# Sums on TensorE in sixteen uneven groups, and two units of a chunk moved from rows to columns

## The reference

```python
e = stack([tbl_f[ids[:, f]] for f in range(32)], axis=1)       # 1024 x 32 x 64
z = einsum('bne,hne,bnh->bn', e[:, ROW], K, e[:, COL])         # 1024 x 496
h = concatenate([z, dense_ctx], axis=1)                        # 1024 x 512
h = maximum(h @ W_top1 + b_top1, 0)                            # 512
h = maximum(h @ W_top2 + b_top2, 0)                            # 256
y = h @ W_top3                                                 # 1
```

## Time and profile before

| | |
|---|---|
| median of three runs | 434.41 us (434.13 to 434.64) |
| time of the profiled execution | 433.44 us |
| its span, first to last instruction | 431.6 us |
| around the span | 1.8 us |
| busy: PE, ACT, DVE, POOL | 386.8, 350.7, 338.0, 242.2 us |
| granted TensorE clock, mean | 0.999 of full speed |

### The profile page before, as it was taken

One profiled execution on the slowest core, in us unless ns is written; L12 is line 12 of the kernel. 1 busy time (PEld: TensorE's weight loads), 2 busy tenths in 40 slices (PEclk: granted clock), 3 DMA queues, 4 the chain that ended last, 5 costly groups with the idle time before them and its releaser, 6 DMA issues.

```text
span 431.6 us, 9783 instructions
## 1 busy us (share of the span) xinstructions
PE 386.8 (90%) x2912; PEld 218.4 (51%) x2912; DVE 338.0 (78%) x369; ACT 350.7 (81%) x2850; POOL 242.2 (56%) x260
## 2 busy tenths in 40 slices
PE   0224789999989999999989999999989999999997
PEld 0113344546454655645554655655555655655556
DVE  1033898999988879699888879699888869799841
ACT  1000799999994999999983999999974999999971
POOL 5777777777777777777777777777770000000000
PEclk9999999999999999999999999999999999999999
DMA  4677992111111111111111111111110000000000
GB/s 120 157 168 162 200 261 58 30 25 29 28 27 29 30 26 30 25 29 30 25 30 30 25 30 29 26 30 25 30 30 2 1 2 1 2 3 0 2 2 0
DMA packets 13637, 19.29 MB, mean 45 GB/s; under 512 B 5584, under 2 KB 6928, under 8 KB 13584
## 3 DMA queue, kind: packets, MB, share of 16 engines
q0 software_dynamic: 8192, 8.40, 10.0%
q1 hardware_dynamic: 5392, 10.27, 10.0%
HBM read 18.65 MB, written 0.00 MB: 43 GB/s over the span
## 4 chain that ended last, share of the span: by engine, by line
PE 66%; ACT 20%; POOL 5%; DVE 3%; issue 3%; DMA 2%; DVEq 0%
PE bil L552 24%; ACT rows_prod L365 19%; PE bil L537 16%; PE z_ps L572 13%; PE side_ps L597 5%; POOL gathered L345 5%; PE side_ps L602 3%; DVE prod L447 2%; PE bil L520 2%; DMA gathered<-in_tbl,ids_sb 1%; PE bil L633 1%; PE z_ps L587 1%; PE bil L657 1%; PE side_ps L607 1%; DVE rows_prod L438 1%
## 5 line engine op out<-in xcount | busy, mean ns | idle before, releaser
L365 ACT ACTIVATE rows_prod<-rows_prod 128x64 f32<-128x64 f32 x1408 | 336.1, 245 | 56.0 <-DVE rows_prod L438 56.0
L345 POOL DMA_INDIRECT gathered<-in_tbl,ids_sb x256 | 242.0, 945 | 80.3 <-issue 77.7
L365 ACT ACTIVATION_READ_ACCUMULATOR rows_prod<-rows_prod 128x1 f32 x1408 | 269.3, 191 | 0.0
L552 PE MATMUL bil<-emb,k_sb 64*128 64x256 f32 x1280 | 163.9, 392 | 6.3 <-DVE emb L426 5.5
L447 DVE TENSOR_TENSOR prod<-bil,emb 128x1024 f32<-128x1024 f32 x128 | 151.3, 1214 | 8.6 <-PE bil L552 8.4
L552 PEld LDWEIGHTS bil<-emb,k_sb 64*128 64x128 f32 x1280 | 120.0, 190 | 65.2 <-issue 38.8
L438 DVE TENSOR_TENSOR rows_prod<-bil,gathered 128x1024 f32<-128x1024 f32 x96 | 115.2, 1215 | 28.2 <-PE bil L537 27.8
L537 PE MATMUL bil<-k_sb,emb 64*128 64x512 f32 x384 | 99.6, 610 | 1.6 <-DVE inner L458 1.6
L572 PE MATMUL z_ps<-prod,sel_sb 128*32 128x512 f32 x576 | 86.0, 604 | 0.2 <-ACT z_sb L375 0.2
L537 PEld LDWEIGHTS bil<-k_sb,emb 64*128 64x128 f32 x384 | 33.5, 186 | 32.0 <-DVE prod L447 16.9
L520 PE MATMUL bil<-ident_sb,gathered 64*128 64x64 f32 x256 | 15.2, 241 | 33.1 <-DMA gathered<-in_tbl,ids_sb 33.1
(11 more groups left out here) (31 smaller groups left out, 72.3 us busy)
## 6 DMA issues: line engine op xcount, KB each, us to landing
k_sb<-in_k_blocks SPq DMA_DIRECT2D x24, 256.0 KB, 4.8
gathered<-in_tbl,ids_sb POOLq DMA_INDIRECT x256, 2.4
k_sb<-in_k_blocks SPq DMA_DIRECT2D x8, 192.0 KB, 5.8
inner<-in_dense_rows SPq DMA_DIRECT2D x64, 1.0 KB
w_sb<-in_w SPq DMA_DIRECT2D x1, 1024.0 KB
k_sb<-in_k_blocks SPq DMA_DIRECT2D x8, 64.0 KB, 4.7
w_sb<-in_w SPq DMA_DIRECT2D x1, 512.0 KB
ids_sb<-in_ids SPq DMA_DIRECT2D x1, 128.0 KB, 2.0
```

Of the source, the lines that this page charges most:

```text
L345: pool.indirect_dma_start(gathered[:, q % 2, t, field * EMBED:(field + 1) * EMBED], None, tables[field], bass.IndirectOffsetOnAxis(ap=ids_ ...
L365: last = act.activation(row, row, ACT.Copy, accum_out=z_rows[:, t, half, col:col + 1])
L552: last = pe.matmul(out[:, s, i * CHUNK:(i + 1) * CHUNK], k_sb[rows, n, :], e[rows, j, :], start=True, stop=True)
```

## The change

Two of the 24 batch units of a chunk become fields units (two units of quad 3), so 42 units are summed on PE and 22 on ACT or DVE. The strings of `ORDER` for the quads 3 to 7 are new. DVE sums one batch unit a chunk (u39, behind u40) in place of two. PE's sums are made in 16 groups of `SUM_GROUPS` units, still behind the third unit after the group's last. Ring waits, the inner units' waits and the bank's two halves are counted by these groups; the first half is complete with the twelfth. The tower's pieces stand at other units.

```diff
-ORDER = ["", "ff", "bbbb", "bfbbfb", "fffbbfff", "bfbbfffbff", "bbffbbffbfbf", "fffbffbbfbffff"]
+ORDER = ["", "ff", "bbbb", "fbfffb", "bffffbff", "bbbfffbfff", "bbbfbfffbffb", "fbbbffbfffffff"]
...
-SUM_UNITS = [8, 52]
+SUM_UNITS = [40]
...
-BATCH_UNITS = 2
-BATCHES = NS // BATCH_UNITS
-GROUP_BATCHES = 32 // BATCH_UNITS
+SUM_GROUPS = [4, 3, 3, 2, 2, 3, 3, 2, 4, 2, 3, 1, 2, 3, 3, 2]
+BATCHES = len(SUM_GROUPS)
+GROUP_ENDS = [sum(SUM_GROUPS[:b + 1]) for b in range(BATCHES)]
+assert GROUP_ENDS[-1] == NS
+GROUP_BATCHES = GROUP_ENDS.index(32) + 1
...
+def group_of(a):
+    q, r = divmod(a, NS)
+    return q * BATCHES + sum(1 for end in GROUP_ENDS if end <= r)
+
+def group_end(b):
+    q, r = divmod(b, BATCHES)
+    return q * NS + GROUP_ENDS[r]
...
 def reduce_unit(b):
-    return unit_at((b + 1) * BATCH_UNITS - 1) + REDUCE_LAG
+    return unit_at(group_end(b) - 1) + REDUCE_LAG
...
-PIECE_UNITS = [9, 14, 32, 56]
+PIECE_UNITS = [10, 31, 40, 54]
...
-            return summed_before(q * NU + FIRST_OF[k]) // BATCH_UNITS
+            return group_of(summed_before(q * NU + FIRST_OF[k]))
...
-                        copy_z(q, b // GROUP_BATCHES)
+                        copy_z(q, int(b == BATCHES - 1))
...
-                    dve.wait_ge(batch_reduced, (a - PROD_RING) // BATCH_UNITS + 1)
+                    dve.wait_ge(batch_reduced, group_of(a - PROD_RING) + 1)
...
             def reduce_batch(b):
-                pe.wait_ge(unit_multiplied, unit_at((b + 1) * BATCH_UNITS - 1) + 1)
+                pe.wait_ge(unit_multiplied, unit_at(group_end(b) - 1) + 1)
                 q, r = divmod(b, BATCHES)
-                if b and r % GROUP_BATCHES == 0:
+                if b and r in (0, GROUP_BATCHES):
                     pe.wait_ge(z_copied, 2 * q + r // GROUP_BATCHES)
-                for a in range(b * BATCH_UNITS, (b + 1) * BATCH_UNITS):
+                for a in range(group_end(b) - SUM_GROUPS[r], group_end(b)):
```

## The result

The changed kernel takes 439.95 us (median; 439.81 to 440.26) against 434.27 of the kernel before on the same chip: a ratio of 1.0133, 95% interval 1.0121 to 1.0146, so 5.7 us slower. The forecast was 442.3, from 437.5 to 445.5.

The account below looks back on a forecast made before the run. PE was taken to bound chunks 1 to 3, with gathers setting chunk 0 until T4. Chunks 0 to 3 add 0.45 + 2.22 + 2.22 + 3.03 = +7.9 us to the 434.41 median: 442.3, range 437.5 to 445.5.

Parts of the forecast that it names:

- PE sets the chunks: Chunks 1 and 2: time is PE's work plus one 1.54 us wait; ACT and DVE have nine and thirteen us spare.
- 25 passes against 20: PE's sums, each chunk: five more passes (four strips side by side, half-empty ones costing 0.87 us too) add 4.35 us.
- Four switches less: PE's sums, each steady chunk: 16 groups against 20 save four tiling switches of 0.33 us, -1.32 us.
- The boundary wait: PE's wait for DVE's copy of T1 between chunks: falls by 0.81 us, leaving about 0.73.
- Chunks 1 and 2: Steady chunks: 3.03 us more PE work less 0.81 us of boundary wait, +2.22 us each.
- chunk 3: Last chunk with the tail: no boundary wait to save, tail behind the last turn unchanged, +3.03 us.
- Chunk 0: First chunk, from T4 to the turn: +2.49 us of passes and switches less 1.05, 0.81 and 0.18 of waits, +0.45.
- the upper bound, 1.5: Chunk 0, seven units without a sum between S7 and S8: up to 1.5 us could be lost to DVE's pace.
- The offset: Whole kernel: the profiled execution lies 0.97 us under the median, assumed the same after the change.
- Half-empty passes cost half: Rival on PE's sums: only switches count, a half-empty pass costs half; faster, 429.1 us; chance 0.08.
- ACT holds chunk 0: Rival: ACT limits chunk 0, so the first turn comes 3.85 us sooner; 438.0 us in all; chance 0.06.
- PE loses step with DVE: Rival: seven-unit runs without a sum, then two passes idling DVE; 1 us in each chunk gives 446; chance 0.08.

Follow-up runs that it names:

- half products: VectorE multiplies only the first bank of each pair, in four kernels: before 431.8 us, changed 438.85, groups of four 426.89, groups of 3, 3, 2 439.86.
- the groups of 3, 3, 2: Kernel before, same order, its 40 summed units a chunk in 15 groups of 3, 3, 2 instead of 20 groups of 2: 452.3 us, ratio 1.0431.
- the groups of four: Kernel before, same order, its 40 summed units a chunk in 10 groups of 4 instead of 20 groups of 2, prod ring of 6: 445.74 us, 1.0266.
- the ring of seven: Kernel before with 10 groups of 4 a chunk and a prod ring of 7 in place of 6: 446.53 us, ratio 1.0272.

## Why the prediction was right, and where its sizes were off

- **PE sets the chunks.** Right, and shown: relief of ACT alone changed nothing, and quick products take 0.05 us from a steady chunk of the changed kernel.
- **25 passes against 20.** Right in kind and nearly in size: a pass with two strips is 0.85 to 0.86, forecast 0.87. The rule on mode switches (the Trainium skill, TensorEngine Tiling (Array Packing), Key Properties) covers only the smaller part, and by it alone the change would have gained.
- **Four switches less.** Right; the size is uncertain. The steady chunk gives 5 x 0.855 - 0.75 - 1.93 = 1.6 for four, 0.40 each, against 0.33. With half products the comparison of the changed kernel with the one before gives (4.28 - 2.75) / 4 = 0.38, the groups of 3, 3, 2 (4.28 - 2.85) / 5 = 0.29, the groups of four 0.28.
- **The boundary wait.** Forecast to fall by 0.81, to 0.73; it fell by 0.75, to 0.79. Of the two reasons given, the row sum (that of u47, made behind u52) was not enough by itself: with the new order and groups of two the wait is 1.14. The longer group ahead of T1 was: with groups of 3, 3, 2 in before's order, the row sum still behind u52, it is 0.79.
- **Chunks 1 and 2** came to +1.92 and +1.93 where +2.22 was forecast, chunk 3 to +2.79 where it was +3.03: the pass and the switch together.
- **Chunk 0** was forecast at +0.45 and came to -0.24. The assumption that failed is that T4 stays at 58.74. In the profiled execution it started at 57.91, with no wait ahead of it:

```profile
56.95 1.03 PE L587 MATMUL z_ps<-prod,sel_sb 128*32 128x512 f32 x4
57.91 0.46 PE L535 MATMUL bil<-ident_sb,gathered 64*128 64x64 f32 x8
```

From there to the turn are 72.47 us against 71.88, +0.59, within 0.15 of the forecast; but that is in part luck. The changed kernel with half products takes 71.07 for the same stretch, with the same wait of 0.79 for T1's copy:

```profile
58.51 0.46 PE L537 MATMUL bil<-ident_sb,gathered 64*128 64x64 f32 x8 [1.67 <-DMA gathered<-in_tbl,ids_sb]
...
129.58 1.06 PE L604 MATMUL z_ps<-ident_sb,z_rows 128*32 128x128 f32 x32
```

So 1.4 of the 72.47 is DVE's pace, which the sum put at nothing and only the upper bound, 1.5, allowed for; 0.7 of it lies between S7 and S8, where the prediction looked for it (6.91 against 6.22 us). What made up for it is not shown: in the kernel before with half products ACT keeps PE waiting in this chunk (1.33 for its copy of the bank, 0.88 at the turn), so before's own share of DVE's pace cannot be read off in the same way.

PE's waits for gathered rows were 31.9 us in four, against 33.1 in five; but the changed kernel with half products, with the same order, has 33.5 in five, so the landing varies between executions and the 0.8 is no merit of the order.
- **The offset.** The forecast for the median carried over that before's profiled execution lay 0.97 under its median. After, it lay 0.14 under (439.81 against 439.95). This is 0.83 of the 2.35 us by which the forecast was high; the span's sum (7.9 against 6.4) is the other 1.5.
- **The rivals.** "Half-empty passes cost half" is out (3 units at 1.84, 4 at 1.85). "ACT holds chunk 0" is out by the run with one unit less on it. "PE loses step with DVE" was given 0.08 for this kernel. In the steady chunks it is indeed absent (0.05 us), in chunk 0 it is 1.4; and it decides the other groupings in before's order: 3.1 us a chunk with 3, 3, 2 and 4.9 with fours. The argument used against it, that l2 behind u40 gives DVE time, was not tested. My expectation of the groups of 3, 3, 2 left it out, that of the groups of four named it only as a rival, and both failed by it.

## What to carry to other kernels

A group of matmuls that are spread over strips cost by the fullest strip here: count passes per strip, not matmuls, and fill them, before counting switches. When an engine makes a long stretch of work that feeds nobody, what counts is whether the ring behind it holds enough for its consumer; if the consumer is slower than the producer's burst that follows, both lose, and the list of waits shows only part of it: look for distances that equal the other engine's pace. An engine that fills the chain of waits may be one that merely arrives at the same moment: look when the other one was ready.

## What the runs showed of the hardware beyond that

In the tail of the changed kernel the last two groups have five units: ten matmuls, of which two strips get two and two get three. PE's timeline:

```profile
422.69 2.34 PE L587 MATMUL z_ps<-prod,sel_sb 128*32 128x512 f32 x18
424.45 0.61 PE L602 MATMUL z_ps<-ident_sb,z_rows 128*32 128x128 f32 x8
424.86 0.60 PE L587 MATMUL z_ps<-prod,sel_sb 128*32 128x512 f32 x2
425.29 1.04 PE L602 MATMUL z_ps<-ident_sb,z_rows 128*32 128x128 f32 x24
```

The turn's first matmuls began at 424.45, before the last records of the sums at 424.86, of which two strips still had a third matmul to do. So the work that follows can begin beside a half-empty pass, if it runs in strips of 32 as well (the rows do not name the strips; that it was the free ones is argued). The units that follow a group inside a chunk do not run so, and there the half pass is lost, as the prices of groups of three and one show. (The Trainium skill, TensorEngine Tiling (Array Packing), Key Properties, has it that tiles work independently of each other; these rows agree.)

The granted clock moved most in the groups of four. With the ring of seven, PE was busy for 2.44 of the five us from 128 to 133, where it waited 2.56 for T1's copy, and the clock granted was 0.79 of the full 2.4 GHz there and 0.87 in the next five; so in part of both it was on the lower level, 1.2 GHz.

```profile
128.00:133.00 5.00, 2.44 (x22) 1.84 (x21) 2.91 (x5) 4.06 (x34) 3.78 (x4) 0.79 0.16 28
133.00:138.00 5.00, 5.00 (x70) 3.08 (x68) 3.26 (x5) 0.34 (x1) 3.78 (x4) 0.87 0.14 26
```

Its chunks are 100.83 and 100.65 at a clock of 0.98, against 99.18 at 1.00 with the ring of six. There the same wait of 2.56 stands at the end of each of the first three chunks; the clock fell behind the first (0.66 from 130 to 135) and stayed at 1.00 behind the other two. The groups of four with half products show what it costs within one execution: the second chunk takes 94.24 at 1.00, the third 95.86 at 0.98, with 2.02 of waiting for T1's copy in both. So such a wait was followed by the lower clock in some cases and not in others, and the fall cost 1.6 us beyond the wait.

```profile
130.00:135.00 5.00, 5.00 (x44) 2.43 (x45) 2.13 (x4) 0.38 (x4) 3.78 (x5) 0.66 0.14 27
```

```profile
223.75:319.61 95.86, 93.84 (x732) 56.98 (x728) 57.25 (x91) 87.43 (x713) 72.40 (x78) 0.98 0.12 28
```

It is no cause of the groups of four being slow, since the chunks at 1.00 were slow without it.
